# Feed-forward blocks of a macaron layer: silu in place of Exp for the softmax over experts, and norms computed a chunk earlier and scaled by ScalarE

## The reference

```python
x = x + 0.5 * ffn(layernorm(x), ...)
x = x + attention(layernorm(x), ...)
x = x + 0.5 * ffn(layernorm(x), ...)      # the same weights as the first

# ffn: a shared swiglu and the two best of 8 experts
logits = x_flat @ router_w
scores = softmax(logits)                               # over 8 experts
_, sel = top_k(scores + expert_bias, 2)
swiglu(x, w1, w2, w3) = (silu(x @ w1) * (x @ w3)) @ w2
out = swiglu(x, shared) + sum over the 2 chosen e of scores[e] * swiglu(x, e)
```

## Time and profile before

| | |
|---|---|
| median of 3 runs | 1307.13 us (1298.42, 1307.13, 1308.70) |
| the profiled execution | 1297.96 us |
| its span, first to last instruction | 1296.1 us |
| TensorE busy | 1144.0 us, 88% |
| VectorE busy | 1053.6 us, 81% |
| ScalarE busy | 815.9 us, 63% |
| GpSimd busy | 548.8 us, 42% |
| granted TensorE clock, mean | 0.977 of 2.4 GHz |

### The profile page before, as it was taken

The page is one execution under the profiler, slowest core; times in us unless marked ns, Lnnn a source line. Parts: engine busy times, 40 slices in busy tenths (PEclk is TensorE's granted clock), DMA queues, the critical chain, the costliest instruction groups (busy, mean ns, idle before and its releaser), DMA issues. The chain is left out here.

```text
span 1296.1 us, 31853 instructions
## 1 busy us (share of the span) xinstructions
PE 1144.0 (88%) x11588; PEld 671.2 (52%) x11588; DVE 1053.6 (81%) x2621; ACT 815.9 (63%) x1477; POOL 548.8 (42%) x658
## 2 busy tenths in 40 slices
PE   3999989898978999999999999999888989899998
PEld 1555555454543555555555555555545555555555
DVE  6878888878876888888788888888578888888876
ACT  4565656565643666677666676677565666666664
POOL 2455555555531333333233333333335555555545
PEclk9999999999986999999999999999989999999999
DMA  5342424242300000000000000000042423333332
GB/s 167 94 147 76 148 75 147 68 126 73 125 8 1 2 2 2 2 1 2 2 2 2 2 2 2 2 2 2 2 132 75 126 97 114 109 93 131 105 118 91
DMA packets 59864, 80.11 MB, mean 62 GB/s; under 512 B 5568, under 2 KB 26944, under 8 KB 59712
## 3 DMA queue, kind: packets, MB, share of 16 engines
q1 hardware_dynamic: 59712, 78.08, 18.9%
HBM read 73.34 MB, written 4.72 MB: 60 GB/s over the span
## 5 line engine op out<-in xcount | busy, mean ns | idle before, releaser
L648 POOL TENSOR_TENSOR h_lo<-h,h_hi 128x512 f16<-128x512 f32 x288 | 333.7, 1159 | 346.0 <-ACT h_hi L606 346.0
L1086 DVE TENSOR_REDUCE neg_max_at<-score_at 128x2 f16<-128x512 f32 (+1 forms) x384 | 254.0, 690 | 71.6 <-PE score_at L917 66.9
L1206 POOL TENSOR_SCALAR_AFFINE_SELECT probs_at<-probs_at 128x512 f32<-128x512 f32 x256 | 156.3, 634 | 345.7 <-ACT probs_at L1164 345.7
L606 ACT ACTIVATE h_hi<-h 128x512 f16<-128x512 f32 x288 | 180.3, 626 | 130.6 <-DVE h L418 111.1
L1164 ACT ACTIVATE probs_at<-prob_at 128x512 f32<-128x512 f32 x384 | 201.7, 599 | 77.9 <-PE prob_at L949 76.0
L408 DVE TENSOR_TENSOR prod<-a,gate_wide 128x512 f32<-128x512 f32 x256 | 176.5, 690 | 75.2 <-ACT a L598 74.0
L536 PE MATMUL y_b<-w_hi,h_hi 128*128 128x128 f16 x1152 | 208.6, 220 | 2.6 <-POOL h_lo L648 2.6
L536 PE MATMUL y_b<-w_hi,h_lo 128*128 128x128 f16 x1152 | 208.7, 220 | 0.0
L536 PE MATMUL y_b<-w_lo,h_hi 128*128 128x128 f16 x1152 | 208.7, 220 | 0.0
L418 DVE TENSOR_TENSOR h<-prod,b 128x512 f32<-128x512 f32 x256 | 175.9, 687 | 5.3 <-issue 0.3
L598 ACT ACTIVATE a<-a 128x512 f32<-128x512 f32 x256 | 148.9, 582 | 43.0 <-PE a L520 42.1
(11 more groups left out here) (134 smaller groups left out, 2006.9 us busy)
## 6 DMA issues: line engine op xcount, KB each, us to landing
gate_wide<-gate_rows SPq DMA_DIRECT2D x256, 256.0 KB, 5.2
x<-in_L_attn_x_dram SPq DMA_DIRECT2D x16, 256.0 KB, 6.3
out_dram<-x SPq DMA_DIRECT2D x16, 256.0 KB, 7.2
raw_w<-in_L_ffn_w_dram SPq DMA_DIRECT2D x3, 512.0 KB, 6.0
gate_rows<-gate_rows SPq DMA_DIRECT2D x32, 16.0 KB, 1.4
raw_w<-in_L_ffn_sw_dram SPq DMA_DIRECT2D x3, 64.0 KB, 4.1
raw_attn<-in_L_attn_W_Q_dram SPq DMA_DIRECT2D x1, 64.0 KB, 5.0
raw_attn<-in_L_attn_W_K_dram SPq DMA_DIRECT2D x1, 64.0 KB, 2.7
```

What stands on the lines that cost most here:

```text
L606: nc.scalar.activation(h_hi[k][:, :], h[k][:, :], ACT.Copy).then_inc(hhi_done, 1)
L648: nc.gpsimd.tensor_tensor(h_lo[k][:, :], h[k][:, :], h_hi[k][:, :], ALU.subtract).then_inc(hlo_done, 1)
L1086: nc.vector.tensor_reduce(dst, src, AX.X, ALU.max, negate=True).then_inc(max_done, 1)
L1206: nc.gpsimd.affine_select(out=p, in_=p, compare_op=ALU.is_ge, fill=0.0, base=0, pattern=[[0, GROUPS], [1, P]], channel_multiplier=-1).then ...
```

## The change

In the feed-forward phases e^z is no longer asked of ScalarE. It computes silu(z) with z = logits - 1 - peak (so z is at most -1), and VectorE makes silu(z) / (z - silu(z)), which is e^z; the factor e^-1 falls out in the softmax. That makes three more gate steps: 22 in place of 19. The gate steps move: 0 and 1 to step 6, 2 to 5 to step 8 of the chunk before, 6 to 21 to steps 0 to 3. `silu_z(c+2)` comes on ScalarE after `silu_a` of step 8.

The statistics of a norm are taken for chunk c+3, two tiles after h of step 5 and two after h of step 6, the moments after h of step 7; GpSimd makes rstd after h_lo of step 7, and with two more small operations shift = -(mean * rstd). In the next chunk ScalarE scales the four tiles with Identity(x * rstd + shift), two after `silu_a` of step 0 and two after that of step 1. `turn_x` and `split_x` move from step 4 to 3, `turn_gates` and the router from 6 to 5, the residual from 3 to 4. In the first chunk, norm(2) stays where it was and its scaling is on ScalarE in step 2. Ahead of the loop of phase 0, scale(0) stands first on ScalarE, and scale(1) between the high parts of w3 and w2; GpSimd makes both roots ahead of the low part of w2. The attention phase keeps its scaling on VectorE.

```diff
-GATE_STEPS = 19
-GATE_PLACES = (2, 2, 2, 4, 6, 8, 10, 12, 14, 16) + (GATE_STEPS,) * (2 * STEPS - 9)
+GATE_STEPS = 22
+GATE_PLACES = (6, 6, 8, 10, 12, 14, 16, 19) + (GATE_STEPS,) * (2 * STEPS - 7)
-GATES_BEGIN = (7, 1)
+GATES_BEGIN = {(6, 1): (0, 2), (8, 0): (2, 4), (8, 1): (4, 6)}
...
+def norm_shift(pool, nc, n, c, buf, rooted, shifted):
+    pool.wait_ge(rooted, 2 * c + 2)
+    nc.gpsimd.tensor_tensor(buf["mean_root"][:, :], buf["moments"][:, :, 0], buf["rstd"][:, :],
+                            ALU.mult).then_inc(shifted, 1)
+    pool.wait_ge(shifted, 2 * n + 1)
+    nc.gpsimd.tensor_scalar(buf["shift"][:, :], buf["mean_root"][:, :], -1.0, None, ALU.mult).then_inc(shifted, 1)
...
                     elif step == 1:
-                        done = nc.vector.tensor_tensor(shifted, logits, wide(top["peak"]), ALU.subtract)
+                        done = nc.vector.scalar_tensor_tensor(z, logits, -1.0, wide(top["peak"]), ALU.add, ALU.subtract)
                     elif step == 2:
+                        done = nc.vector.tensor_tensor(below, z, g["silu_z"], ALU.subtract)
+                    elif step == 3:
+                        done = nc.vector.reciprocal(below, below)
+                    elif step == 4:
+                        done = nc.vector.tensor_tensor(g["expd"], g["silu_z"], below, ALU.mult)
+                    elif step == 5:
                         done = nc.vector.tensor_reduce(top["total"][:, :], g["expd"], AX.X, ALU.add)
...
             def chunk(c):
                 for e in range(STEPS):
                     swiglu(c, e)
-                    if e == 0 and c + 2 < CHUNKS + 2 * more:
-                        norm(c + 2)
-                    if e == 2 and c + 2 < CHUNKS + 2 * more:
-                        scale(c + 2)
-                    if e == 3 and c > 0:
+                    if c == 0 and e == 0:
+                        norm(2)
+                    if e == 3 and c + 2 < CHUNKS + more:
+                        split_x(c + 2)
+                    if e == 4 and c > 0:
                         residual(c - 1)
-                    if e == 4 and c + 2 < CHUNKS + more:
-                        split_x(c + 2)
+                    if e in (5, 6) and has_norm(c + 3):
+                        stats(c + 3, range(2 * e - 10, 2 * e - 8))
+                    if e == 7 and has_norm(c + 3):
+                        norm_moments(dve, nc, norm0 + c + 3, buf, ln_step)
                     beside(c, e, 1)
...
+            def scale(c, tiles=range(TILES)):
+                act.wait_ge(shifted, 2 * (c - 2 * made) + 2)
+                wait_count(act, xt_done, c - made)
+                for t in tiles:
+                    last = nc.scalar.activation(xn[:, t, :], chunk_rows(x, c)(t), ACT.Identity,
+                                                scale=buf["rstd"][:, t:t + 1], bias=buf["shift"][:, t:t + 1])
...
-            def expd(c):
+            def silu_z(c):
                 act.wait_ge(gate_step, c * GATE_STEPS + 2)
-                nc.scalar.activation(g["expd"], g["shifted"][:, :, :], ACT.Exp).then_inc(expd_done, 1)
+                nc.scalar.activation(g["silu_z"], g["z"][:, :, :], ACT.Silu).then_inc(silu_z_done, 1)
...
                     silu_a(c, e)
                     if c == 0 and e == 1:
                         take_gates(0)
-                        expd(1)
-                    if c > 0 and e == 0 and c + 1 < CHUNKS:
-                        expd(c + 1)
-                    if e == 4 and c + 2 < CHUNKS + more:
+                        silu_z(1)
+                    if e == 8 and c + 2 < CHUNKS:
+                        silu_z(c + 2)
+                    if c == 0 and e == 2:
+                        scale(2)
+                    if e < 2 and c > 0 and has_norm(c + 2):
+                        scale(c + 2, range(2 * e, 2 * e + 2))
+                    if e == 3 and c + 2 < CHUNKS + more:
                         split_x(c + 2)
...
+            if not made:
+                scale(0)
             if prepare:
                 prepare.high(act, "router")
...
                 prepare.high(act, "w3")
+                scale(1)
                 prepare.high(act, "w2")
-            expd(0)
+            silu_z(0)
...
             if not made:
-                norm_root(pool, nc, 0, buf, ln_step, ln_rooted)
+                root(0)
+                root(1)
             if prepare:
                 prepare.low(pool, nc.gpsimd, "w2")
-            if not made:
-                norm_root(pool, nc, 1, buf, ln_step, ln_rooted)
```

More of the change, by code:

```diff
@@ L68, in chunk_rows, with norm_stats, norm_moments @@
     return lambda t: x[:, first + t, :]
[L71 to L76, removed]
+def norm_stats(dve, nc, c, rows, buf, step, scaled, tiles=range(TILES)):
+    if tiles[0] == 0:
+        wait_count(dve, scaled, c)
+    for t in tiles:
         nc.vector.bn_stats(buf["stats"][:, t, :], rows(t)).then_inc(step, 1)
-    dve.wait_ge(step, base + TILES)
+def norm_moments(dve, nc, c, buf, step):
+    dve.wait_ge(step, c * LN_STEPS + TILES)
     nc.vector.memset(buf["spare"][:, :], 0.0)
@@ L243, in ffn_phase @@
         gate_rows = sb("gate_rows", [EXPERTS * TILES, P], F32)
-        g = {n: sb(n, [P, TILES, EXPERTS], F32) for n in ("shifted", "first", "chosen")}
+        g = {n: sb(n, [P, TILES, EXPERTS], F32) for n in ("z", "below", "first", "chosen")}
         gate = sb("gate", [P, EXPERTS, TILES], F32)
@@ L251, in ffn_phase @@
         y_bank = [bank(f"y_b{s}") for s in range(2)]
-        for i, n in enumerate(("logits", "expd", "score", "biased", "hit", "rank", "rest", "second")):
+        for i, n in enumerate(("logits", "silu_z", "expd", "score", "biased", "hit", "rank", "rest", "second")):
             g[n] = r_bank[:, i * TILES * EXPERTS:(i + 1) * TILES * EXPERTS].rearrange("p (t e) -> p t e", e=EXPERTS)
@@ L266, in ffn_phase, with has_norm @@
             sem(n) for n in ("hhi_done", "hlo_done", "w2_done", "x_added", "stored"))
+        shifted = sem("shifted")
+        def has_norm(c):
+            return c < CHUNKS + 2 * more
         block = ctx.enter_context(nc.Block())
@@ L312, in _, with stats @@
         def _(dve):
-            def norm(c):
+            def stats(c, tiles=range(TILES)):
                 if c >= CHUNKS:
@@ L317, in norm @@
                     dve.wait_ge(x_loaded[c % 2], (c // 2 + 1) * DMA)
[L318 to L322, removed]
+                norm_stats(dve, nc, norm0 + c, chunk_rows(x, c), buf, ln_step, ln_done, tiles)
+            def norm(c):
+                stats(c)
+                norm_moments(dve, nc, norm0 + c, buf, ln_step)
             def split_x(c):
@@ L335, in gates @@
                 order = consts["order"][:, :].unsqueeze(1).to_broadcast([P, TILES, EXPERTS])
-                shifted, first_hit, chosen = (g[n][:, :, :] for n in ("shifted", "first", "chosen"))
+                z, below, first_hit, chosen = (g[n][:, :, :] for n in ("z", "below", "first", "chosen"))
                 for step in range(first, last):
@@ L390, in beside @@
                     gates(c + 1, at[2 * e + place], at[2 * e + place + 1])
-                if c + 2 < CHUNKS and (e, place) == GATES_BEGIN:
-                    gates(c + 2, 0, 2)
+                if c + 2 < CHUNKS and (e, place) in GATES_BEGIN:
+                    gates(c + 2, *GATES_BEGIN[e, place])
             def swiglu(c, e):
@@ L442, in _ @@
                 norm(0)
-                scale(0)
             if prepare:
@@ L454, in _ @@
                 norm(1)
-                scale(1)
             gates(0, 0, GATE_STEPS)
@@ L642, in _, with root @@
         def _(pool):
+            def root(c):
+                norm_root(pool, nc, norm0 + c, buf, ln_step, ln_rooted)
+                norm_shift(pool, nc, c - 2 * made, norm0 + c, buf, ln_rooted, shifted)
             def low_part(c, e):
@@ L652, in chunk @@
                     low_part(c, e)
-                    if e == 0 and c + 2 < CHUNKS + 2 * more:
-                        norm_root(pool, nc, norm0 + c + 2, buf, ln_step, ln_rooted)
+                    if c == 0 and e == 0:
+                        root(2)
+                    if e == 7 and has_norm(c + 3):
+                        root(c + 3)
             if prepare:
```

56 lines of the change are left out of this document (31 added, 25 removed).

## The result

| | before | after |
|---|---|---|
| median | 1302.78 us (1296.93 to 1308.70, 4 runs) | 1249.26 us (1246.44 to 1251.15, 4 runs) |
| profiled execution, its span | 1297.96, 1296.1 us | 1246.44, 1244.0 us |
| a usual chunk | 22.03 us | 19.69 us |
| table loads in the kernel | 64 | 4 |

Ratio 0.9587, 95% interval 0.953 to 0.9644: faster by 4.1%. The forecast was 1214 us with a range of 1203 to 1238, so some 35 us of the forecast gain are missing.

A forecast was written before the change was run, and what follows sets the result against it. Chunks were taken as bound first by ScalarE's table loads, then by VectorE, and by TensorE only in the last three steps. 1297.96 - 93.1 (chunks) + 6.7 (heads) = 1211.6 us, forecast as 1214, range 1203 to 1238.

The forecast's parts named there:

- The step that failed: ScalarE in step 0: silu, scaling and h_hi end at 2.85 us, next silu wanted at 2.81, late by 0.04.
- The paragraph on GpSimd: Root between h_lo of steps 7 and 8 takes 1.85 us; h_lo of step 8 ends at 4.4, due 5.2.
- The sign of being wrong: Chunk starts 19.5 us or more apart with TensorE waiting for h, loads inside chunks, or x transposes awaiting xn.
- Table loads: Around Exp at chunk heads: both ScalarE loads go, 2.57 us, and with them 1.99 us of idle VectorE.
- the rival on Identity: Identity is not under Silu's table, so loads return in steps 0 and 1: 1327 us, slower; chance 0.04.
- The floor of 18.54 us: TensorE alone in a usual chunk: nine steps of 1.965 us plus transposes of 0.43 and 0.42.
- the slack of VectorE: In a chunk, 1.7 us of lateness cost TensorE nothing; the worst, in step 3, is 0.8.
- its load: VectorE in a usual chunk: 17.2 us busy, 17.7 with remaining idle time, 0.8 below TensorE's floor.
- Prices: Single operations: scaling on ScalarE 0.5 us, reciprocal of 32 elements 0.4, GpSimd's root with two new operations 1.85.
- The heads: Starts of the phases: later or longer gate chains cost 5.1 us in phase 0, 1.6 in phase 1, together 6.7.
- VectorE as the bound: Rival: each of a chunk's eight pairs costs 0.25 us more in waits; chunk 19.7 us, kernel 1240; chance 0.16.
- the 9 us: Median above the profiled execution, place unknown: gone if in VectorE's scalings, staying and giving 1221 us if in attention.

The follow-up runs named there:

- Runs 1: Changed kernel with ScalarE's scalings one step later, in steps 1 and 2 instead of 0 and 1: 1212.27 us.
- 2: Changed kernel with one more pow of 1.04 us on GpSimd, its result unread, between rstd and shift: 1281.8 us.
- 10: Changed kernel with GpSimd's root and shift ahead of h_lo of step 7, scalings left in steps 0 and 1: 1215.38 us.
- run 8: Run 1's kernel with the first gate silu ahead of scale(1) and w2's high part on ScalarE in phase 0's head: 1209.63 us.
- Run 9: Run 8's kernel with chunk 1's gate steps spread over steps 0 to 3 of chunk 0 and turn_gates(1) in step 5: 1207.39 us.
- runs 3: Kernel before with silu for Exp and its 22 gate steps alone, norms and their scalings unchanged on VectorE: 1261.4 us.
- kernel 4: Changed kernel with Exp and 19 gate steps in place of silu, norms still earlier and scaled by ScalarE: 1288.33 us.

## Why the prediction was wrong, by its own steps

**The step that failed** is the one that asks whether ScalarE holds up the next silu: "0.85 until silu, 0.5 silu, 1.0 scaling, 0.5 h_hi = 2.85". It starts the scaling at 1.35 us into the chunk, as if its operand were there. The paragraph on GpSimd has the operand's time by its own working: h_lo of step 8 "ends 4.4 us into the next chunk" behind the root, so the root ends at 4.4 - 1.16 = 3.24. The two numbers were never held against each other. Done right, with the same terms: scaling from 3.24 to 4.24, h_hi to 4.74, h_lo to 5.9, due at 5.2: 0.7 late a chunk, 1231 us in all (1211.6 + 28 x 0.7). Measured: shift at 3.58, h_hi from 4.39, h_lo ends at 6.25, 1.05 after 5.2, and TensorE's step is 1.16 longer. The sum lists what is queued behind the scaling (h_hi, then the next silu), but it puts the scaling's own wait at nothing, without a reason; that wait measured 2.16 us. Runs 1, 2 and 10 show the mechanism from three sides: take the wait away, lengthen it, take it away elsewhere. The sign of being wrong that the prediction gave, "starts 19.5 or more apart with TensorE waiting for h", came half: the starts are 19.69 apart, but TensorE waits for h_lo.

**Table loads**: right. Four are left where 64 were, none in a chunk, and the copies and Identity run under Silu's table; the rival on Identity is out. The sentence "what is late next is nothing of ScalarE" was wrong: what came next was ScalarE standing idle.

**The floor of 18.54 us** was right: kernels 1 and 10 run at 18.53 or 18.54. So were the slack of VectorE (no prod or h keeps TensorE waiting in the chunk although step 3 holds 3 us of VectorE's work) and its load: 17.2 forecast, 16.38 measured.

**Prices**: a scaling was to take 0.5 us; it takes 0.48, and a pair 0.88, so 0.40 from start to start. The reciprocal of 32 was to take 0.4 and takes 0.35. The root and its two new operations were to take 1.85 and take 189.55 - 187.63 = 1.92.

**The heads** were to cost 6.7 us: phase 0 3.28 (49.34 against 46.06) where 5.1 was forecast, phase 1 1.5 where 1.6 was. The late gates of chunk 0 are the cause in phase 0, as run 8 shows (4.15 us back). They end at 25.26, 2.9 later than before where 4.2 was forecast, mostly since norm 1 is scaled from 16.31 on and not from 17.25. (The prediction names 2.9 as well, but for a table load that lies earlier; the load stands where it assumed, so that is luck.) The longer chain of chunk 1 counts as forecast: it ends at 33.50, and the first prod starts with its end, at 33.40 (34.7 forecast). Run 9, in which that chain costs nothing, has the reads of gate_wide as the later of the two; it says nothing on the changed kernel.

**VectorE as the bound**: the time of this rival, 1240 us and 19.7 us a chunk, is close to what was measured, but its mechanism is false, since VectorE has 3.3 us to spare and the chunk gets shorter by an edit that gives VectorE no less work. A matching total is no evidence for a mechanism.

**The two halves apart** (runs 3 and 4) were worth 3.1% and 1.0%, and each alone leaves its own bound: VectorE's load in one, ScalarE's loads and its wait for the shift in the other.

## What to carry to other kernels

When work moves to an engine that works through its queue in order, write down two times for each moved instruction: when the engine gets to it and when its last operand is ready. If the second is later, everything queued behind it slips by the difference, and if the operand's own producer waits for something in that queue, the delay returns to the path. Where such a wait is found, moving the waiting instruction behind the urgent ones, or its producer ahead of its neighbour, can be worth more than half of what the change itself brings: here 37 us in the medians (1249.26 to 1212.27), against 54 for the whole change (1302.78 to 1249.26). VectorE's scaling of SBUF data should be priced beside what GpSimd does at that time, not alone.

## What was not expected of the hardware

**Attention, in unchanged code, takes 504.0 to 512.8 us** from its first to its last inv_at, over twelve profiled executions (before 504.5, after 508.5, kernel 4 512.2). The windows of kernel 4 show TensorE's granted clock in it: the whole of attention, then ten microseconds of it, then three stretches of two.

```profile
425.60:937.80 512.20, 467.09 (x5542) 272.91 (x5534) 413.99 (x908) 347.62 (x694) 168.88 (x278) 0.97 0.01 2
...
585.60:595.60 10.00, 10.00 (x84) 5.18 (x77) 5.44 (x10) 4.02 (x9) 1.91 (x4) 0.56 0.01 2
...
581.00:583.00 2.00, 0.98 (x8) 0.35 (x8) 0.70 (x1) 1.88 (x4) 0.76 (x2) 1.00 0.00 0
...
585.00:587.00 2.00, 2.00 (x21) 0.78 (x19) 1.34 (x3) 0.67 (x2) 1.22 (x2) 0.50 0.00 0
```

At 581 us TensorE is busy for 0.98 of 2.00 us at the full 2.4 GHz; then the grant falls, to 0.50 (1.2 GHz) by 585, and is back at 1.00 by 595. VectorE, ScalarE and GpSimd have the same busy time in attention as in the kernel before (413.99, 347.62, 168.88 against 413.41, 347.61, 168.83). This is where the profiled executions lie apart from each other, and it is likely what the 9 us were that the prediction could not place. Runs without a trace have their mean granted clock on record: 27 later executions of the kernel before go from 1295.74 us at 0.980 to 1309.40 at 0.966, and the longer ones have the lower clock nearly throughout. The profiled one has 1297.96 at 0.977. In which phase the longer runs lost their clock isn't recorded. Whether the change can influence it at all wasn't tried.

**A scaling on VectorE varies fourfold for one instruction**, 0.33 us alone and up to 1.24 us beside GpSimd's h_lo, while prod and h, of four times the elements, take 0.63 to 0.69. The kernel before had this hidden in a group of four that took 2.31 us in most chunks and 1.11 in a few.
